# A 32-byte SBUF tensor is allocated ahead of the attention tensors instead of behind them, in a gated-attention and expert kernel

## The chip, the cores and the metric

The kernel runs as one program on one core of a Trainium2 chip. Its time is the device time of one execution in microseconds. Three executions took 1172.36, 1173.41 and 1173.3 us, median 1173.3 us.

## The reference: what is computed

`x` and `ctx_1024` are (8, 512, 512) float32: 8 batches of 512 rows, width 512. Two blocks follow each other, each added to its input.

```python
def xattn(char_emb, subword_emb, ...):            # char_emb = layernorm(x), subword_emb = ctx
    scores   = (char_emb Wq_c + bq_c)(subword_emb Wk_s + bk_s)^T / sqrt(512)
    char2sub = softmax(scores) (subword_emb Wv_s + bv_s)
    scores2  = (subword_emb Wq_s + bq_s)(char_emb Wk_c + bk_c)^T / sqrt(512)
    sub2char = softmax(scores2) (char_emb Wv_c + bv_c)
    gate = sigmoid([char2sub, sub2char] Wg^T + bg)
    return gate * char2sub + (1 - gate) * sub2char

def ffn(x, router_w, router_b, expert_w, expert_b):  # x = layernorm(x1), 4096 tokens, 8 experts
    probs = softmax(xt @ router_w + router_b)
    gate, idx = max(probs), argmax(probs)
    return gate * (xt @ expert_w[idx] + expert_b[idx])

x1  = x  + tanh(g_xattn) * xattn(layernorm(x), ctx, ...)
out = x1 + tanh(g_ffn)   * ffn(layernorm(x1), ...)
```

## The kernel before, in words

**Precision.** Every large product is made of three float32r matmuls, high times high, high times low and low times high (`PASSES`, L41, in `product`, L153 to L163). So each tensor that TensorE multiplies stands in SBUF as a pair of a high and a low part; ScalarE writes the high part out of PSUM, VectorE the low one.

**Stages.** First the query and key weights are multiplied with one another (`weights_part`), while the first rows of `x` are loaded into the tensor that the profile calls `pairs_as_f` (L689, L882). Four more weights follow, 128 rows at a time, through the two halves of `x1_tile` (L898 to L903). Then come 8 batches, the middle ones in a hardware loop; the order of each engine's work in a batch is written out by hand in `steps_of_a_batch` (L473 to L538). A batch has two directions of attention, each with four steps Q (queries), V (values), S (scores), PT (transposed probabilities) and U (the attended sum), then the gate product G, the mix M, and the router. Steps marked `prev` belong to the batch before, those marked `nxt` to the next one. Behind the last batch 39 tiles of 128 tokens go each through its own expert (`experts_part`): POOL gathers the rows of a tile from DRAM (L1617), SP loads the expert's bias, one row broadcast to 128 partitions (L1565), ScalarE normalises (L1655), TensorE transposes and multiplies (L1795, L160), VectorE adds (L1763, L1771), and POOL scatters the tile to the output (L1624).

**SBUF.** The program allocates SBUF tensors one behind the other in the order of the calls `sb(...)`, each rounded up to a multiple of 32 bytes per partition. Tensors opened on `top` keep their place to the end. The first group is the `arena` (nine slots for pairs of 512 by 512), constants, `in_tile` (three rows buffers of 2112 bytes), `junk`, `bn_x` and `mv_x` (L90 to L114). `attention_part` opens a second group behind them: `q_pair`, `c2s_pair`, `probs`, `x1_tile`, `diff`, `normed`, `normed_t`, then `row_next`, `bn_1`, `stats` and the small rest (L596 to L619). Two further names are other views of the same bytes: `pairs_as_f32` (L117) is opened and closed where `q_pair` and `c2s_pair` come to lie, and `experts_part` cuts its buffers out of these, of `probs`, of `in_tile` and of an arena slot (L1520 to L1531).

**The tensor of the change.** `row_next` has 8 float32 per partition. VectorE writes one element of it as the accumulated result of a dot product of a row with a vector, in steps XD (L1309 to L1311) and CD (L1316 to L1318), and copies all of it into `row_const` once in a batch (L1259). No other engine touches it.

**Who sets the order.** Semaphores alone: each step waits for counts that others raise. No scheduler or planner looks at the addresses.

Of the kernel before, what the change touches and what calls it, by code (L numbers as in the profile page):

```python
# [32 lines left out]
P = 128  # L33
B, L, H, E = 8, 512, 512, 8
C = H // P
T = L // P
# [37 lines left out]
def gated_attention_and_experts(nc, x, ctx_in, g_xattn, g_ffn, Wq_c, bq_c, Wk_s, bk_s, Wv_s, bv_s,  # L74
                                Wq_s, bq_s, Wk_c, bk_c, Wv_c, bv_c, Wg, bg, router_w, router_b,
                                expert_w, expert_b, out):
    x_rows = x.rearrange("b l h -> (b l) h")
    c_rows = ctx_in.rearrange("b l h -> (b l) h")
    out_rows = out.rearrange("b l h -> (b l) h")

    x1_dram = nc.dram_tensor("x1_rows", (N + 1, ROWX), F32, kind="Internal").ap()
    x1_early = nc.dram_tensor("x1_rows_early", (N - L, ROWX), F32, kind="Internal").ap()
    list_dram = nc.dram_tensor("token_lists", (SLOTS, LINE), I32, kind="Internal").ap()

    with ExitStack() as top:
        def sb(name, shape, dt=F32):
            return top.enter_context(nc.sbuf_tensor(name, shape, dt))


        k = Shared()  # L90
        with ExitStack() as scope:
            k.slot_as_f32 = [scope.enter_context(nc.sbuf_tensor(f"slot{i}_as_f32", [P, 2, C, H], F32)) for i in range(9)]
        k.arena = sb("arena", [P, 9, 2, C, H], F32R)
        k.ident = sb("ident", [P, P])
        k.ones_bf = sb("ones_bf", [P, P], BF16)
        k.before_bf = sb("before_bf", [P, P], BF16)
        k.u_row = sb("u_row", [P, 2, H])
        k.u_const = sb("u_const", [P, 2])
        k.c_col = sb("c_col", [P, 2, C])
        k.bv_col = sb("bv_col", [P, 2, C])  # L100
        k.bg_half = sb("bg_half", [P, C])
        k.tanh_g = sb("tanh_g", [P, 2])
        k.router_parts = sb("router_parts", [P, C, PARTS, E], BF16)
        k.router_b = sb("router_b", [P, E])
        k.rank_of_e = sb("rank_of_e", [P, E])
        k.list_start = sb("list_start", [P, E])
        k.list_end = sb("list_end", [P, E])
        k.tile_no = sb("tile_no", [P, TILES])
        k.minus_half = sb("minus_half", [P, 1])
        k.token_ids = sb("token_ids", [P, T + LINE - 1], I32)  # L110
        k.in_tile = sb("in_tile", [P, 3, ROWX])
        k.junk = sb("junk", [P, H], BF16)
        k.bn_x = sb("bn_x", [P, 6])
        k.mv_x = sb("mv_x", [P, 2, 3])  # L114


        with nc.sbuf_tensor("pairs_as_f32", [P, 2, 2 * C * L], F32) as pairs_as_f32:  # L117
            k.pairs_as_f32 = pairs_as_f32
        k.mm_bank, k.tr_bank, k.u_bank = (
            [top.enter_context(nc.psum_tensor(f"{name}{i}", [P, 512], F32)) for i in range(n)]  # L120
            for name, n in (("mm", 2), ("tr", 2), ("u", C)))
        weights = weights_part(nc, top, k, x1_dram, list_dram,
                               dict(Wq_c=Wq_c, bq_c=bq_c, Wk_s=Wk_s, bk_s=bk_s, bv_s=bv_s, Wq_s=Wq_s,
                                        bq_s=bq_s, Wk_c=Wk_c, bk_c=bk_c, bv_c=bv_c, bg=bg, g_xattn=g_xattn,
                                        g_ffn=g_ffn, router_w=router_w, router_b=router_b))
        with ExitStack() as scope:
            attention = attention_part(nc, scope, top, k, x_rows, c_rows, x1_dram, x1_early, list_dram, expert_w,
                                       (Wg[:, 0:H], Wv_s, Wv_c, Wg[:, H:2 * H]), weights)
        experts = experts_part(nc, top, k, x1_dram, x1_early, list_dram, out_rows, expert_b, attention)

        with nc.Block(no_gpsimd_drain=True) as block:
            @block.sync
            def _(sp):
                attention.sync(sp, weights.sync(sp), experts.sync(sp))

            @block.scalar
            def _(act):
                attention.scalar(act, weights.scalar(act), experts.scalar(act))

            @block.vector  # L140
            def _(dve):
                attention.vector(dve, weights.vector(dve), experts.vector(dve))

            @block.gpsimd
            def _(pool):
                attention.gpsimd(pool, weights.gpsimd(pool), experts.gpsimd(pool))

            @block.tensor
            def _(pe):
                attention.tensor(pe, weights.tensor(pe), experts.tensor(pe))  # L150
# [429 lines left out]
def attention_part(nc, scope, top, k, x_rows, c_rows, x1_dram, x1_early, list_dram, expert_w,  # L580
# [3 lines left out]
    bg_half, tanh_g, router_parts = k.bg_half, k.tanh_g, k.router_parts  # L584
    rank_of_e, list_end = k.rank_of_e, k.list_end
    minus_half, token_ids, in_tile = k.minus_half, k.token_ids, k.in_tile
    junk, bn_x, mv_x = k.junk, k.bn_x, k.mv_x

    def sb(name, shape, dt=F32):
        return scope.enter_context(nc.sbuf_tensor(name, shape, dt))  # L590
# [10 lines left out]
    diff = sb("diff", [P, H])  # L601
    normed = sb("normed", [P, H])
    normed_t = sb("normed_t", [P, 2, C, P], BF16)
    row_next = sb("row_next", [P, 2, T])
    bn_1 = sb("bn_1", [P, 6])
    stats_flat = sb("stats", [P, 4 * T + LINE - 4])
    stats = stats_flat[:, 0:4 * T].rearrange("p (t s) -> p t s", s=4)
# [1239 lines left out]
```

## Time and profile before

| | |
|---|---|
| median of 3 runs | 1173.3 us (1172.36 to 1173.41) |
| the profiled execution | 1172.36 us |
| its span, first to last instruction | 1170.6 us |
| outside the span | 1.76 us |
| TensorE busy | 1149.4 us, 98% of the span |
| VectorE, ScalarE, GpSimd busy | 712.3, 458.5, 212.8 us |
| granted TensorE clock, mean | 0.995 |

PE is TensorE's matmuls, PEld its weight loads, DVE VectorE, ACT ScalarE, POOL GpSimd, SP the engine that issues most DMAs. A name such as `x_tile` or `pairs_as_f` is the program's name with digits at the end of a part left out, so `x_tile` is `x1_tile`. A tensor that is seen through an alias is listed by the alias: the buffers of the expert stage appear as `pairs_as_f` (on the place of `q_pair` and `c2s_pair`) and as `slot_as_f` (on the arena). The share of DMA is the mean busy share of the core's 16 DMA engines.

### The profile page before, as it was taken

What the parts mean: (1) busy time and instruction counts of PE and PEld (TensorE: products, weight loads), DVE (VectorE), ACT (ScalarE), POOL (GpSimd) and SP (SyncE); (2) the same over time, 40 slices, a digit from 0 to 9 for tenths busy, and PEclk for the clock granted to TensorE, in tenths of its full rate; (3) what the DMA queues carried; (4) which work ended last, traced back from release to release, by engine and by line L of the source; (5) the groups of instructions that cost most, each with busy time, mean ns of one, the idle gap of its engine ahead of it and who ended that gap; (6) DMA issues with size and microseconds to landing.
All of it is one profiled execution on the core that took longest, in us unless ns stands there. A gap on an engine that the chain in (4) does not pass through costs nothing.

```text
span 1170.6 us, 18120 instructions
## 1 busy us (share of the span) xinstructions
PE 1149.4 (98%) x5937; PEld 944.7 (81%) x5937; DVE 712.3 (61%) x1497; ACT 458.5 (39%) x812; POOL 212.8 (18%) x339
## 2 busy tenths in 40 slices
PE   7999999999999999999999999999999999998998
PEld 6778888888888888888888888888888888877776
DVE  5765646565557545763566466646565658788565
ACT  5533423442344324432344244423442355544342
POOL 3300001010002100110011011201020101256664
PEclk8999999999999999999999999999999999999999
DMA  6042113010202020101101120102010312586683
GB/s 235 28 164 65 35 28 102 8 49 27 99 9 48 27 77 30 39 25 65 54 21 36 41 85 21 36 27 99 9 39 1 135 46 76 200 263 195 182 253 121
DMA packets 59445, 90.64 MB, mean 77 GB/s; under 512 B 20523, under 2 KB 21063, under 8 KB 59401
## 3 DMA queue, kind: packets, MB, share of 16 engines
q1 hardware_dynamic: 49232, 64.25, 18.0%
q0 software_dynamic: 7264, 19.20, 4.9%
q10 hardware_dynamic: 2904, 6.63, 1.5%
q8 instruction: 24, 0.39, 0.1%
q14 instruction: 21, 0.16, 0.0%
HBM read 62.77 MB, written 29.12 MB: 78 GB/s over the span
## 4 chain that ended last, share of the span: by engine, by line
PE 92%; issue 2%; DVE 2%; ACT 2%; another core or an unknown queue 1%; DMA 1%; POOL 1%; SPq 0%; POOLq 0%; DVEq 0%; ACTq 0%
PE mm L160 58%; PE u L1016 15%; PE tr L968 8%; PE u L160 7%; PE mm L1795 1%; PE tr L160 1%; PE tr L1070 1%; DVE arena L1238 1%; ACT pairs_as_f L1655 0%; DMA slot_as_f<-in_L_xattn_Wk_s 0%; ACT slot_as_f L281 0%; DMA x_tile<-in_L_xattn_Wv_s 0%; DVE arena L416 0%; POOL slot_as_f L346 0%
## 5 line engine op out<-in xcount | busy, mean ns | idle before, releaser
L160 PE MATMUL mm<-arena 128*128 128x512 f32 x1536 | 376.1, 396 | 1.9 <-DVE arena L1238 1.8
L160 PEld LDWEIGHTS mm<-arena 128*128 128x128 f32 x1536 | 284.3, 189 | 59.5 <-DVE arena L1238 2.2
L1016 PE MATMUL u<-arena 128*128 128x512 f32 x768 | 189.9, 398 | 0.0
L160 PE MATMUL mm<-arena,q_pair 128*128 128x512 f32 x768 | 183.8, 394 | 0.0
L160 PEld LDWEIGHTS mm<-arena,q_pair 128*128 128x128 f32 x768 | 141.7, 188 | 28.8
L1016 PEld LDWEIGHTS u<-arena 128*128 128x128 f32 x768 | 140.0, 188 | 27.5
L1238 DVE TENSOR_TENSOR arena<-tr,arena 128x512 fp32r<-128x512 f32 x144 | 96.3, 685 | 37.0 <-ACT arena L1131 16.9
L1238 DVE TENSOR_TENSOR arena<-mm,arena 128x512 fp32r<-128x512 f32 x64 | 44.2, 691 | 93.3 <-ACT arena L1122 89.2
L1118 ACT ACTIVATE q_pair<-mm,c_col 128x512 fp32r<-128x512 f32 x64 | 44.1, 689 | 125.9 <-PE mm L160 122.0
L1239 DVE SCALAR_TENSOR_TENSOR q_pair<-mm,c_col,q_pair 128x512 fp32r<-128x512 f32 x64 | 48.1, 751 | 72.9 <-ACT q_pair L1118 71.3
L1122 ACT ACTIVATE arena<-mm 128x512 fp32r<-128x512 f32 x64 | 38.3, 599 | 129.2 <-PE mm L160 129.2
L160 PE MATMUL mm<-c2s_pair,arena 128*128 128x512 f32 x360 | 87.2, 392 | 0.0
L160 PE MATMUL mm<-q_pair,arena 128*128 128x512 f32 x360 | 86.4, 389 | 0.0
L1127 ACT ACTIVATE probs<-mm,neg_top 128x512 f32<-128x512 f32 x64 | 44.2, 691 | 103.3 <-DVE neg_top L1265 95.0
L1422 POOL TENSOR_SCALAR mv_x<-mv_x 128x1 f32<-128x1 f32 x32 | 13.9, 435 | 381.7 <-DVE mv_x L1305 381.6
L160 PE MATMUL u<-arena,q_pair 128*128 x312 | 79.5, 405 | 1.9 <-DVE q_pair L1756 1.6
L160 PEld LDWEIGHTS mm<-q_pair,arena 128*128 128x128 f32 x360 | 67.6, 188 | 14.0
L160 PEld LDWEIGHTS mm<-c2s_pair,arena 128*128 128x128 f32 x360 | 67.1, 188 | 13.8
L1422 POOL TENSOR_SCALAR stats<-stats 128x1 f32<-128x1 f32 x32 | 7.9, 248 | 356.2 <-DVE stats L1337 356.0
L1284 DVE SCALAR_TENSOR_TENSOR probs<-probs,u 128x512 f32<-128x512 f32 x32 | 22.0, 687 | 79.7 <-ACT probs L1154 79.5
L160 PEld LDWEIGHTS u<-arena,q_pair 128*128 128x128 f32 x312 | 57.9, 192 | 13.9 <-issue 2.4
L1154 ACT ACTIVATE probs<-mm,bg_half 128x512 f32<-128x512 f32 x30 | 20.7, 690 | 123.6 <-PE mm L160 123.6
(213 smaller groups left out, 1558.6 us busy)
## 6 DMA issues: line engine op xcount, KB each, us to landing
in_tile<-in_ctx SPq DMA_DIRECT2D x31, 256.0 KB, 2.6
x_tile<-in_x SPq DMA_DIRECT2D x29, 256.0 KB, 2.6
x_rows<-x_tile SPq DMA_DIRECT2D x29, 256.0 KB
in_tile<-in_x SPq DMA_DIRECT2D x28, 256.0 KB, 2.7
x_rows_early<-x_tile SPq DMA_DIRECT2D x28, 256.0 KB, 2.3
probs<-in_L_ffn_expert_b SPq DMA_DIRECT2D x21, 256.0 KB
slot_as_f<-in_L_ffn_expert_w SPq DMA_DIRECT2D x4, 1024.0 KB, 5.2
slot_as_f<-in_L_ffn_expert_w ACTq DMA_DIRECT2D x3, 1024.0 KB, 8.9
```

Of the source, the lines that this page charges most:

```text
L160: last = pe.matmul(bank, lhsT(a, c), rhs(b, c), start=start and n == 0, stop=stop and n == C * len(PASSES) - 1)
L968: last = pe.transpose(bank[:, tile(n)], block_of(n), ident[:])
L1016: last = pe.matmul(u_bank[m][:], v_pair[:, i % 2, a, tile(m)], pt_pair[:, i % 2, p], start=i == 0 and n == 0, stop=i == T - 1 and n == 2)
L1070: last = pe.matmul(bank[:, 0:n * E], part_of_rows(i, part)[:, c], router_parts[:, c, 0:n].rearrange("p n e -> p (n e)"), start=c == 0 and ...
L1118: act.activation(q_pair[:, HI, i], bank[:], ACT.Identity, bias=c_col[:, d, i:i + 1]).then_inc(q_hi, 1)
L1122: act.activation(v_pair[:, i % 2, HI], bank[:], ACT.Copy).then_inc(v_hi, 1)
L1127: act.activation(probs[:, i], bank[:], ACT.Exp, bias=neg_top[:, d, i:i + 1], scale=SCALE, accum_out=p_sum[:, d, i:i + 1]).then_inc(exp_don ...
L1154: act.activation(probs[:, i], bank[:], ACT.Tanh, bias=bg_half[:, i:i + 1], scale=0.5).then_inc(tanh_done, 1)
L1238: return dve.tensor_tensor(to, bank, f32(hi), ALU.subtract)
L1239: return dve.scalar_tensor_tensor(to, bank, bias, f32(hi), ALU.add, ALU.subtract)
L1284: dve.scalar_tensor_tensor(mix, mix, 1.0, u_bank[i][:], ALU.subtract, ALU.mult).then_inc(nd_used, 1)
L1422: then(pool.tensor_scalar(rstd, var, EPS, None, ALU.add))
```

## The change

The call that allocates `row_next` moves from `attention_part`, where it stood behind `normed_t`, to the end of the first group, behind `mv_x`. `attention_part` takes it from there by its name.

```diff
@@ gated_attention_and_experts
         k.bn_x = sb("bn_x", [P, 6])
         k.mv_x = sb("mv_x", [P, 2, 3])
+        k.row_next = sb("row_next", [P, 2, T])
@@ attention_part
-    junk, bn_x, mv_x = k.junk, k.bn_x, k.mv_x
+    junk, bn_x, mv_x, row_next = k.junk, k.bn_x, k.mv_x, k.row_next
@@
     normed_t = sb("normed_t", [P, 2, C, P], BF16)
-    row_next = sb("row_next", [P, 2, T])
     bn_1 = sb("bn_1", [P, 6])
```

On every engine the same instructions stand in the same order as before, with the same shapes, waits and semaphores; only line numbers below L114 are one higher. What differs is the byte address, within each partition, of eight allocations (and of the alias `pairs_as_f32`):

| tensor | bytes | address before | address after | before, modulo 64 | after, modulo 64 |
|---|---|---|---|---|---|
| `q_pair`, `pairs_as_f32` | 16384, 32768 | 177280 | 177312 | 0 | 32 |
| `c2s_pair` | 16384 | 193664 | 193696 | 0 | 32 |
| `probs` | 8192 | 210048 | 210080 | 0 | 32 |
| `x1_tile` | 4096 | 218240 | 218272 | 0 | 32 |
| `diff` | 2048 | 222336 | 222368 | 0 | 32 |
| `normed` | 2048 | 224384 | 224416 | 0 | 32 |
| `normed_t` | 2048 | 226432 | 226464 | 0 | 32 |
| `row_next` | 32 | 228480 | 177280 | 0 | 0 |

All else stays: the arena at 16512, `in_tile` at 169856 (its three buffers begin at 0, 64 and 0 modulo 128), `bn_x` at 177216, `mv_x` at 177248, `bn_1` at 228512, and the small tensors behind it, among them `mx` at 228704 (32 modulo 64) and `neg_top` at 228736 (0 modulo 64). Before the change every one of the large tensors in the table begins at a multiple of 128 bytes, and so does each of the 2048-byte rows in them.

## Rows read from the trace of the kernel before

**Rows 1.** The page's head: span, and busy time of each engine.
```profile
span 1170.6 us, 18120 instructions
PE 1149.4 (98%) x5937; PEld 944.7 (81%) x5937; DVE 712.3 (61%) x1497; ACT 458.5 (39%) x812; POOL 212.8 (18%) x339
```
**Rows 2.** The chain that ended last, share of the span by engine.
```profile
PE 92%; issue 2%; DVE 2%; ACT 2%; another core or an unknown queue 1%; DMA 1%; POOL 1%; SPq 0%; POOLq 0%; DVEq 0%; ACTq 0%
```
**Rows 3.** Busy time by stretch; columns in the first row.
```profile
core 0: us, PE busy (x) PEld busy (x) DVE busy (x) ACT busy (x) POOL busy (x), PEclk, DMA share, GB/s
0.00:50.00 50.00, 42.19 (x195) 33.82 (x195) 32.66 (x59) 29.66 (x51) 19.96 (x42) 0.93 0.43 148
50.00:130.00 80.00, 78.64 (x394) 64.38 (x395) 50.69 (x112) 32.38 (x63) 1.66 (x4) 1.00 0.28 94
490.00:610.00 120.00, 120.00 (x631) 99.19 (x629) 69.65 (x151) 43.90 (x79) 12.81 (x28) 1.00 0.15 44
1000.00:1050.00 50.00, 48.87 (x253) 40.36 (x252) 40.57 (x66) 26.16 (x44) 18.80 (x22) 1.00 0.72 239
1050.00:1100.00 50.00, 44.09 (x252) 34.86 (x251) 35.77 (x83) 20.26 (x33) 32.23 (x32) 0.97 0.64 190
1100.00:1150.00 50.00, 49.30 (x245) 39.81 (x243) 32.68 (x47) 20.93 (x32) 31.88 (x31) 1.00 0.81 239
```
**Rows 4.** TensorE in order of time, gate and next Q: start, us, what.
```profile
288.57 2.88 PE L160 MATMUL mm<-c2s_pair,arena 128*128 128x512 f32 x12
291.29 2.88 PE L160 MATMUL mm<-q_pair,arena 128*128 128x512 f32 x12
294.01 8.33 PE L160 MATMUL mm<-arena 128*128 128x512 f32 x36
302.18 1.03 PE L968 MATMUL tr<-ident,probs 128*128 128x128 f32 x8
```
**Rows 5.** Matmul groups that read the shifted pairs: busy us, mean ns.
```profile
L160 PE MATMUL mm<-arena,q_pair 128*128 128x512 f32 x768 | 183.8, 394 | 0.0
L160 PE MATMUL mm<-c2s_pair,arena 128*128 128x512 f32 x360 | 87.2, 392 | 0.0
L160 PE MATMUL mm<-q_pair,arena 128*128 128x512 f32 x360 | 86.4, 389 | 0.0
```
**Rows 6.** Instructions on in_tile and pairs_as_f: ns min/median/max, first and last start.
```profile
L968 PEld LDWEIGHTS tr<-ident,in_tile x236: 137/139/143, 44.3 to 888.3; 128*128 128x128 f32 x118
L1655 ACT ACTIVATE pairs_as_f<-in_tile x21: 801/806/814, 1016.6 to 1158.2; 128x512 f32<-128x512 f32 x21
L1655 ACT ACTIVATE pairs_as_f<-pairs_as_f x18: 803/807/813, 1030.6 to 1148.6; 128x512 f32<-128x512 f32 x18
```
**Rows 7.** VectorE on small tensors, and what touches row_next.
```profile
L1263 DVE SCALAR_TENSOR_TENSOR mx<-mx,row_const 128x1 f32<-128x1 f32 x64 | 10.2, 159 | 2.2
L1265 DVE TENSOR_TENSOR neg_top<-row_const,mx 128x1 f32<-128x1 f32 x64 | 10.2, 160 | 2.2
L1309 DVE DVE_READ_ACCUMULATOR2_ANT row_next<- x32: 76/81/84, 44.2 to 891.0; 128x1 f32 x32
```
**Rows 8.** DMA issues: tiles, engine, count, KB each, us to landing.
```profile
in_tile<-in_ctx SPq DMA_DIRECT2D x31, 256.0 KB, 2.6
x_tile<-in_x SPq DMA_DIRECT2D x29, 256.0 KB, 2.6
probs<-in_L_ffn_expert_b SPq DMA_DIRECT2D x21, 256.0 KB
pairs_as_f<-in_L_ffn_expert_b SPq DMA_DIRECT2D x12, 256.0 KB
in_tile<-x_rows_early,u_row POOLq DMA_INDIRECT x11
pairs_as_f<-x_rows_early,u_row POOLq DMA_INDIRECT x9
```
**Rows 9.** Pieces of the chain in the expert stage.
```profile
1082.00 6.65 another core or an unknown queue
1096.80 3.46 another core or an unknown queue
```

## The prediction

> **What bounds the kernel now.** I read the page's head first, then the chain of waits, then the busy time by stretch, and last the single groups that touch what the change moves. The head says that TensorE is busy in 1149.4 us of a span of 1170.6 us [rows 1]. The chain agrees: 92% of it is TensorE [rows 2]. By stretch the reader is to see three regimes [rows 3]. From 0 to 50 us TensorE is busy for 42.19 us, from 50 to 130 us for 78.64 of 80 us. In the batches it has no gap at all (120.00 us of 120.00 between 490 and 610 us), with the DMA engines busy for only 0.15. From 1000 us the expert stage has few gaps but busy DMA engines: shares of 0.72, 0.64 and 0.81, and TensorE at 48.87, 44.09 and 49.30 of 50 us. So two things could move the end: a change in what a matmul costs, anywhere, or a change in what a transfer costs, in the expert stage. Everything else has cover.
>
> How matmuls follow one another is read from their starts, not from their durations, which overlap (the groups' means are 389 to 394 ns [rows 5]). Twelve matmuls with `c2s_pair` as moving operand start at 288.57, the next twelve, with `q_pair`, at 291.29, and the 36 that take both operands from the arena at 294.01 and end where the transposes start, at 302.18 [rows 4]. That is 2.72 us for 12, or 226.7 ns each, twice, and 8.17 us for 36, or 226.9 ns each. The pace is one and the same whatever tensor is streamed.
>
> **The change part by part.** No instruction is removed, added or reordered, and no wait changes. There are three things to price.
>
> (a) `row_next` itself moves. It is written by VectorE's accumulator reads (81 ns in the median of 32 [rows 7]) and copied once in a batch. These are writes of 4 bytes, and VectorE is busy for only 69.65 us of 120 in a batch's stretch [rows 3]. The nearest rows for the position of a small tensor are two operations on one element per partition: the one that writes `mx`, which begins at 32 modulo 64, takes 159 ns, the one that writes `neg_top`, at 0 modulo 64, takes 160 ns [rows 7]. The bound is 1 ns either way on 60 writes, 0.06 us, beside TensorE's work. I take 0. If the cover were gone it would still be 0.06 us.
>
> (b) The compute engines read and write `q_pair`, `c2s_pair`, `probs`, `x1_tile`, `diff`, `normed` and `normed_t` at 32 modulo 64 where it was 0. For VectorE and ScalarE I have rows at 0 and 64 modulo 128, since the three buffers of `in_tile` begin at both: ScalarE's normalisation out of it takes 801 to 814 ns over 21 cases, against 803 to 813 ns out of and into the aligned `pairs_as_f`, and TensorE's weight loads from it 137 to 143 ns over 236 [rows 6]. A residue by itself shows no effect there. No large tensor stands at 32 modulo 64 in this trace, so the price has to be bounded. The end above: if a row of 2048 bytes were fetched in pieces of 64 bytes, the shifted row would touch 33 of them where it touched 32, 1/32 more. For the 720 matmuls that stream `c2s_pair` or `q_pair` [rows 5] that is 720 x 226.7 / 32 = 5.1 us, all of it on the path, since TensorE has no gap there. The 768 that take `q_pair` as weights [rows 5] hide it: a weight load on `in_tile` is 139 ns [rows 6] beside a pace of 227 ns. The end below is a gain: in the gate product both operands begin at multiples of 128 now, so if that cost anything the shift would save it. But 226.7 and 226.9 ns are equal within 0.2 ns, with pairs of one kind or the other, and 0.2 x 720 = 0.14 us is what the rows let it be. Between +5.1 and -0.14 us I take 0, because every row that could show a dependence on the place shows none.
>
> (c) DMAs land in and leave shifted tensors. In the batches these are the residual loads and the stores of `x1_tile` at a DMA share of 0.15: loads into the aligned `x_tile` and into `in_tile`, with buffers at both residues, land in the same 2.6 us [rows 8]. They are issued several microseconds ahead and TensorE waits for none of them, so even a landing one half longer would cost nothing. At 50 to 130 us sixteen weight loads pass through `x1_tile`; the whole idle time of TensorE there is 1.36 us [rows 3]. In the expert stage a tile moves 264 KB of gathered rows, 256 KB of bias and 256 KB of output. Of the 39 biases 21 land in `probs` and 12 in `pairs_as_f` [rows 8], of the gathers those into `pairs_as_f` (9 from the early copy [rows 8] and 9 more), the output leaves the arena and does not move. So (33/39 x 256 + 18/39 x 264) / 776 = (217 + 122) / 776 = 0.44 of the bytes have a shifted end. The end below is 0. The end above, if a shifted packet took twice as long: the share of 0.81 becomes 0.81 x 1.44 = 1.17, and 50 us would need 58.3; 0.72 becomes at most 1.04, and 0.64 stays under 1 [rows 3]. That is +8.3 + 1.8, about +10 us at most. I take 0, as nothing shows such a price.
>
> By the Trainium skill, "DMA: Bandwidth & Descriptors", section on how a descriptor splits into AXI transactions, a source that does not begin at a multiple of 256 bytes is fetched from the boundary below it, in beats of 32 bytes. These rows begin 128 bytes past such a boundary before and 160 after, so by that rule a 2048-byte row read from SBUF costs 69 beats where it cost 68, 1.5% more, an estimate from the page. No row here shows a packet at the new residue, so the trace neither agrees nor disagrees. By the rule the sum would stay 0, but it speaks for a small price and against the doubling, and I lower the chance of the transfer case for it.
>
> **The sum.** Span 1170.6 + 0 + 0 + 0 = 1170.6 us, and 1.76 us around it make 1172.36, the profiled execution. The median of the runs is 0.94 us above that execution, so the forecast in the terms of the median is 1173.3 us.
>
> **The rivals.**
> *The transfers pay (slower).* Packets with a shifted end take much longer, and the expert stage, whose DMA engines are the busiest resource after TensorE, becomes bound by them. It decides from the point at which 0.81 x (1 + 0.44 a) = 1, a = 0.53: below a half more per packet the stretch of 1100 to 1150 us still fits. At a = 1 it costs +8.3 us there, 1181.6 us. For it: the share of 0.81, and two places where the chain hangs on something late at 1082 and 1096 us [rows 9]. Against it: in the rows at 0 and 64 modulo 128 there is no difference at all [rows 8].
> *The matmul stream pays (slower).* The 1/32 of (b), +5.1 us, 1178.4 us. For it: it would be on the path in full. Against it: it supposes pieces of 64 bytes, and TensorE's pace of 226.7 ns is the same in all streams [rows 4].
> *The late waits of the expert stage fall otherwise (faster).* Two pieces of the chain there, 6.65 and 3.46 us, are no engine's work [rows 9], and TensorE is idle for 5.9 us between 1050 and 1100 us [rows 3]. These come from how gathers, index loads and scatters meet in the queues. If the shift moves landings enough that the larger one doesn't occur, most of the 5.9 us comes back: say 4 us, 1169.3 us. Against it: with packet times unchanged there is nothing to move them, and the same lateness could as well grow.
> *The change does nothing of what it says.* It does move the addresses, but if addresses carry no price this is the forecast itself.
>
> **How the numbers follow.** I give the forecast 0.67: for it are all three prices of zero and an instruction stream that is the same. Transfers 0.10, the matmul stream 0.07, the faster expert stage 0.10, and 0.06 for a drift just past 0.2%, half to each side. A measurement of this kernel can tell about 0.2% (2.3 us) from no change. So faster 0.10 + 0.03 = 0.13, same 0.67, slower 0.10 + 0.07 + 0.03 = 0.20. The forecast's own range is 1171.5 to 1175 us. To hold 8 in 10 the range reaches to 1169.5, at the faster case, and to 1178.5, over the matmul case, and leaves out the doubled transfers.
>
> **What would show it.** In the profile after, the twelve-matmul groups of the gate should still start 2.72 us apart (a stream that pays shows 2.80), ScalarE's instruction of L1655, one line lower, should stay at 806 ns, loads into `x_tile` should land in 2.6 us, and the DMA share between 1100 and 1150 us should stay near 0.81. The forecast is wrong if TensorE's busy time changes by more than 2 us, if landings in shifted tensors lengthen while those in `in_tile` do not, or if the gaps of the expert stage change by more than 2.3 us.

## The result: slower by 0.8%, and the profile after

The changed kernel took 1184.59 us (median of 4 runs, 1183.26 to 1185.67) against 1173.36 us for the kernel before (4 runs, 1172.36 to 1174.52). The ratio is 1.0083 with a 95% interval of 1.0069 to 1.0096; it rests on all 21 executions of the changed kernel, whose median is 1182.87 us, so it is smaller than the quotient of the two medians just given (1.0096). The forecast was 1173.3 us, the range 1169.5 to 1178.5 us: the time lies outside. The profiled execution after took 1182.02 us, 9.66 us more than the one before (1172.36 us).

The page's head of the changed kernel, first the span, then busy time by engine, answers to [rows 1]:

```profile
span 1180.3 us, 18120 instructions
PE 1157.9 (98%) x5937; PEld 944.6 (80%) x5937; DVE 714.0 (60%) x1497; ACT 458.1 (39%) x812; POOL 209.5 (18%) x339
```

The instruction counts are the same. TensorE's busy time has grown by 8.5 us, the span by 9.7 us, and the other engines have stayed within 3.3 us. The granted clock is the same, 0.995 in the mean. By stretch, beside [rows 3] (columns: TensorE busy, weight loads, VectorE, ScalarE, GpSimd, clock, DMA share, GB/s):

```profile
490.00:610.00 120.00, 120.00 (x626) 98.32 (x625) 68.78 (x147) 43.47 (x79) 12.14 (x28) 1.00 0.13 42
1000.00:1050.00 50.00, 49.34 (x239) 40.40 (x238) 36.45 (x61) 24.20 (x41) 15.02 (x16) 1.00 0.61 194
1050.00:1100.00 50.00, 42.00 (x254) 33.03 (x254) 38.40 (x91) 21.66 (x35) 32.75 (x36) 0.97 0.67 212
1100.00:1150.00 50.00, 50.00 (x248) 40.90 (x247) 31.95 (x46) 19.52 (x30) 30.37 (x31) 1.00 0.79 236
```

TensorE had no gap in the batches before and has none now, at a granted clock of 1.00 both times, and yet 626 matmuls stand in 120 us where 631 stood. The stage of the experts comes about 9 us later than before, so its stretches don't hold quite the same work; none of them is bound by transfers. The DMA share from 1100 to 1150 us is 0.79, where it was 0.81, and TensorE has no gap there. Over the whole span TensorE's idle time is 22.4 us where it was 21.2 us (span less busy time). So most of the 9.7 us is matmuls of some kind that take longer. Which kind is read from the starts in order of time. This is the gate and what follows in the second batch, to be laid beside [rows 4] (start, us, what):

```profile
290.61 2.96 PE L161 MATMUL mm<-c2s_pair,arena 128*128 128x512 f32 x12
293.41 2.96 PE L161 MATMUL mm<-q_pair,arena 128*128 128x512 f32 x12
296.21 8.36 PE L161 MATMUL mm<-arena 128*128 128x512 f32 x36
304.41 1.03 PE L968 MATMUL tr<-ident,probs 128*128 128x128 f32 x8
308.83 11.44 PE L161 MATMUL mm<-arena,q_pair 128*128 128x512 f32 x48
```

Twelve matmuls that stream `c2s_pair` or `q_pair` against weights from the arena now start 2.80 us apart from the next twelve, 233.3 ns each, where it was 2.72 us and 226.7 ns. The 36 with both operands in the arena take 8.20 us from start to start, 8.17 before. The transposes of `probs`, which is also shifted, take 1.03 us for 8 as in [rows 4]. The 48 matmuls of the scores, with weights from `q_pair` and a stream from the arena, are slower too, 11.44 us. In the same view of the kernel before:

```profile
306.58 11.17 PE L160 MATMUL mm<-arena,q_pair 128*128 128x512 f32 x48
```

The pieces of the chain of waits (start, us) give the length of a batch, before and then after:

```profile
277.80 24.54 PE mm L160 x108
399.97 24.54 PE mm L160 x108
```
```profile
279.57 25.00 PE mm L161 x108
402.82 25.00 PE mm L161 x108
```

The 48 scores take 0.27 us more (11.44 against 11.17 us), 5.6 ns each. The same piece, 72 matmuls of the gate and the 36 behind them, comes back after 123.25 us where it came after 122.17 us: each batch is 1.08 us longer. Eight batches make 8.6 us.

**The sum of it.** The busy time of whole groups, beside [rows 5], gives what each kind costs over the run:

```profile
L161 PE MATMUL mm<-arena,q_pair 128*128 128x512 f32 x768 | 187.4, 399 | 0.0
L161 PE MATMUL mm<-c2s_pair,arena 128*128 128x512 f32 x360 | 89.3, 397 | 0.0
L161 PE MATMUL mm<-q_pair,arena 128*128 128x512 f32 x360 | 88.7, 395 | 0.0
```

The scores have grown from 183.8 to 187.4 us, by 3.6 us. That is less than 16 x 0.27 = 4.3 us, since only one direction's 48 run unbroken; the other direction's are cut up by transposes. The gate's two groups have grown by 2.1 and 2.3 us. To them belong 48 more gate matmuls of the last batch, which [rows 5] does not list, as they write to another PSUM bank. In the kernel before:

```profile
L160 PE MATMUL tr<-q_pair,arena 128*128 128x512 f32 x24 | 5.9, 395 | 0.0
L160 PE MATMUL tr<-c2s_pair,arena 128*128 128x512 f32 x24 | 5.6, 389 | 0.0
```

They now take 6.0 and 5.8 us. So the gate is 768 matmuls and costs 4.7 us more. The 468 matmuls of the expert stage with weights from the pairs have gone from 118.6 to 119.5 us, by 0.9 us. Together that is 9.2 us of the 9.7 us in the span; the batches' 8.6 us and the experts' 0.9 us make 9.5 us. Nothing else of size is needed. The rest stands where it stood: the weight loads of the scores and the gate take 188 ns before and after, ScalarE's instruction has a median of 808 ns (806 before), VectorE's reads of the accumulator one of 82 ns (81), and the loads into `in_tile` and `x1_tile` land in 2.6 us as before.

(In the changed kernel only lines 115 to 603 are one higher than before; from 604 on the numbers are the old ones. So ScalarE's instruction is still at L1655.)

### The profile page after: what moved, and what is told of

Same layout as the page of the kernel before. It is cut to its first block, busy times and chain, and to the rows that moved or that the text cites. A ratio compares the mean times of both kernels' runs of the same rounds, so it can differ in the third digit from the quotient of the medians.

```text
span 1180.3 us, 18120 instructions
## 1 busy us (share of the span) xinstructions
PE 1157.9 (98%) x5937; PEld 944.6 (80%) x5937; DVE 714.0 (60%) x1497; ACT 458.1 (39%) x812; POOL 209.5 (18%) x339
## 4 chain that ended last, share of the span: by engine, by line
PE 92%; DVE 3%; issue 2%; ACT 1%; DMA 1%; POOL 1%; SPq 0%; DVEq 0%; POOLq 0%; ACTq 0%
PE mm L161 58%; PE u L1016 15%; PE u L161 8%; PE tr L968 7%; PE mm L1795 1%; PE tr L161 1%; PE tr L1070 1%; DVE arena L1238 1%; DMA slot_as_f<-in_L_xattn_Wk_s 0%; DVE arena L417 0%; ACT slot_as_f L282 0%; DVE slot_as_f L1771 0%; DVE arena L401 0%; DMA x_tile<-in_L_xattn_Wv_s 0%; DVE slot_as_f L395 0%
## 5 line engine op out<-in xcount | busy, mean ns | idle before, releaser
L161 PE MATMUL mm<-arena,q_pair 128*128 128x512 f32 x768 | 187.4, 399 | 0.0
L1261 DVE TENSOR_REDUCE mx<-mm 128x1 f32<-128x512 f32 x64 | 44.3, 691 | 43.3 <-PE mm L161 40.0
```

The source lines that it names most:

```text
L161: last = pe.matmul(bank, lhsT(a, c), rhs(b, c), start=start and n == 0, stop=stop and n == C * len(PASSES) - 1)
L1261: then(dve.reduce_max(mx[:, d, i:i + 1], bank[:], axis=AX))
```

## The experiments

Two theories at the start. **A**: a row that does not begin at a multiple of 64 bytes costs TensorE time by itself, in the stream or as weights. **B**: only the distance between the place of the stream and that of the weights counts. The rival behind both was that transfers or other engines pay for the shifted tensors. "Distance" below is the address of the pairs less that of the arena, against the kernel before, where all rows of both begin at 128 modulo 256.

**all_32.** Everything is shifted by 32 bytes together (in the code cuts below, the removal of the old call is left out).

```diff
+        k.row_next = sb("row_next", [P, 2, T])
         with ExitStack() as scope:
             k.slot_as_f32 = ...
         k.arena = sb("arena", [P, 9, 2, C, H], F32R)
```

> row_next stands ahead of the arena, so the arena, in_tile and the pairs all begin at 32 modulo 64; the tensors of one matmul share their place again. Theory A (each 2048-byte or 512-byte row that begins off a multiple of 64 bytes costs 16 more cycles of TensorE's clock, whatever the other operand does): every one of the 4356 matmuls of 512 columns pays at least 6.7 ns, +29 us or more, 1202 us or above; Q steps slow from 2.72 us for 12 matmuls to 2.80 or more. Theory B (it is the difference in place between the operand that is streamed and the one that is loaded as weights that costs): no difference is left, 1173 us, 12 matmuls in 2.72 us everywhere.

Measured: 1173.09 us (10 runs), ratio 0.9986 (0.9975 to 0.9997) to 20 new runs of the kernel before (median 1174.74 us). The gate and the scores, in order of time:

```profile
287.93 2.88 PE L161 MATMUL mm<-c2s_pair,arena 128*128 128x512 f32 x12
290.65 2.88 PE L161 MATMUL mm<-q_pair,arena 128*128 128x512 f32 x12
305.95 11.17 PE L161 MATMUL mm<-arena,q_pair 128*128 128x512 f32 x48
```

2.72 us for twelve, though none of the tensors that TensorE multiplies here stands at a multiple of 64. Theory A is out, and it was A that the prediction's rival had priced. The move of `row_next` itself is out too, since it moves here as well.

**arena_32.** `row_next` ahead of the arena and `bn_1` behind `mv_x`: the arena at 32 modulo 64, the pairs back on a multiple of 64, 32 bytes between them.

> The arena and in_tile begin at 32 modulo 64, the pairs and everything behind them at 64 modulo 128. Theory A: Q, V and U pay with both operands, G as weights and S as the stream, again +27 us or more, about 1200 us; of the single-operand cases S should show 2.80 us for 12 (the streamed operand pays) and G about 2.78 (the weights pay). Theory B: only S, G and the expert products pay, as in the changed kernel, so 1183 to 1185 us, with Q, V and U at 2.72 us for 12.

Measured: 1182.42 us (4 runs), ratio 1.0061 (1.0044 to 1.0078). The same view:

```profile
289.57 2.96 PE L162 MATMUL mm<-c2s_pair,arena 128*128 128x512 f32 x12
292.37 2.96 PE L162 MATMUL mm<-q_pair,arena 128*128 128x512 f32 x12
295.17 8.36 PE L162 MATMUL mm<-arena 128*128 128x512 f32 x36
307.79 11.44 PE L162 MATMUL mm<-arena,q_pair 128*128 128x512 f32 x48
```

The same 2.80 us and 11.44 us as in the changed kernel, while Q and V, both of whose operands are now shifted, pay nothing. B holds, A would have asked for 1200 us.

**rest_32.** The pairs stay, the rest is shifted.

```diff
     c2s_pair = sb("c2s_pair", [P, 2, C, L], F32R)
+    row_next = sb("row_next", [P, 2, T])
     probs = sb("probs", [P, T, L])
```

> row_next stands between c2s_pair and probs: the pairs stay at multiples of 128, and only probs, x1_tile, diff, normed and normed_t are shifted by 32 bytes. Both theories on TensorE's operands say 1173 us, within 0.2%. The rival, that transfers into and out of shifted tiles or the other engines pay, says that a good part of the 10 us is here: 1178 us or more.

Measured: 1174.08 us (10 runs), ratio 0.9991 (0.9979 to 1.0002). The shift of `probs`, `x1_tile`, `diff`, `normed` and `normed_t`, with every transfer into and out of them, costs nothing that can be measured. The transfers into the two pairs are not in this run; they are in all_32, which is no slower either.

**pairs_64.** The changed kernel with `bn_1` behind `row_next`: distance 64.

> As the changed kernel, with 32 more bytes ahead of q_pair, so that q_pair, c2s_pair, probs, x1_tile, diff and normed are shifted by 64 bytes against the kernel before. If the unit is 64 bytes (both theories in their first form): 1173 us and 2.72 us for 12 matmuls of the gate. If the unit is 128 bytes or the shift itself costs: 1183 to 1185 us.

Measured: 1179.91 us (5 runs, 1178.0 to 1182.14), ratio 1.0041 (1.0024 to 1.0057), between the two answers that were expected.

```profile
291.08 2.91 PE L162 MATMUL mm<-c2s_pair,arena 128*128 128x512 f32 x12
293.82 2.91 PE L162 MATMUL mm<-q_pair,arena 128*128 128x512 f32 x12
309.20 11.45 PE L162 MATMUL mm<-arena,q_pair 128*128 128x512 f32 x48
```

Here the two kinds part: the gate's groups are 2.74 us apart, near the old 2.72, and the scores take 11.45 us, as in the changed kernel. So the unit is not 64 bytes. In the gate the stream lies above the weights, in the scores below them, so the sign of the distance may be what parts them. That is not isolated: the two steps also read in a different order, and at 32 bytes both signs cost nearly the same.

**pairs_16, pairs_96, pairs_128, pairs_256.** In the first the two pairs are slices of one allocation, 16 bytes in; in the others two, three and seven more small tensors (`bn_1`, `row_const`, `mx`, ...) are allocated behind `row_next`. Of the edit for 16 bytes the cut shows the main part; `pairs_as_f32` moves with it, and two small tensors are joined.

```diff
-    q_pair = sb("q_pair", [P, 2, C, L], F32R)
-    c2s_pair = sb("c2s_pair", [P, 2, C, L], F32R)
+    both = sb("both_pairs", [P, 4 * C * L + 8], F32R)
+    q_pair, c2s_pair = (both[:, 4 + n * 2 * C * L:4 + (n + 1) * 2 * C * L].rearrange(...) for n in range(2))
```

> q_pair and c2s_pair are slices of one allocation, 16 bytes past a multiple of 128; probs and what follows is at 32 modulo 64, which cost nothing where it was tried alone. The difference in place between the arena and the pairs is 16 bytes. If only the difference modulo 64 or 128 counts and each difference but zero costs about the same: 1183 us, 12 matmuls of the gate in 2.80 us. If the cost grows with the difference and 32 is its height: between 1176 and 1181 us. If differences below 32 bytes are free: 1174 us and 2.72 us.

> row_next, bn_1 and row_const stand ahead of q_pair: pairs and what follows is 96 bytes on. Difference to the arena 96 bytes, that is 32 modulo 64 and -32 modulo 128. If the unit is 64 bytes: as the changed kernel, 1183 us and 2.80 us for 12 matmuls of the gate. If differences count modulo 128 with their sign, the cost can be another: between 1174 and 1190 us.

> row_next, bn_1, row_const and mx stand ahead of q_pair: pairs and what follows is 128 bytes on. If the cost repeats every 128 bytes: 1174 us and 2.72 us for 12, as before. If it follows the difference over a longer stretch: another time, 1177 us or more, and a pace in the gate or the scores other than 226.7 ns.

> Eight small tensors stand ahead of q_pair: pairs and what follows is 256 bytes on. If the cost repeats every 128 or 256 bytes: 1174 us and 2.72 us for 12. If the shift of 128 bytes costs and this one doesn't, the period is 256; if both cost, it is longer. No theory says that this one is cheap and the one of 128 bytes is dear unless the period is 256.

TensorE in order of time at distances 16, 96, 128 and 256, a piece of the gate and then the score step:

```profile
284.83 9.66 PE L160 MATMUL mm<-both_pairs,arena 128*128 128x512 f32 x41
294.33 8.35 PE L160 MATMUL mm<-arena 128*128 128x512 f32 x36
...
306.92 11.13 PE L160 MATMUL mm<-arena,both_pairs 128*128 128x512 f32 x48
```
```profile
292.48 2.96 PE L163 MATMUL mm<-c2s_pair,arena 128*128 128x512 f32 x12
295.28 2.96 PE L163 MATMUL mm<-q_pair,arena 128*128 128x512 f32 x12
310.69 11.49 PE L163 MATMUL mm<-arena,q_pair 128*128 128x512 f32 x48
```
```profile
290.55 2.95 PE L164 MATMUL mm<-c2s_pair,arena 128*128 128x512 f32 x12
293.34 2.94 PE L164 MATMUL mm<-q_pair,arena 128*128 128x512 f32 x12
308.74 11.40 PE L164 MATMUL mm<-arena,q_pair 128*128 128x512 f32 x48
```
```profile
289.48 2.88 PE L168 MATMUL mm<-c2s_pair,arena 128*128 128x512 f32 x12
292.20 2.88 PE L168 MATMUL mm<-q_pair,arena 128*128 128x512 f32 x12
307.49 11.17 PE L168 MATMUL mm<-arena,q_pair 128*128 128x512 f32 x48
```

All distances in one table. The gate column is the step from the start of one group of 12 to that of the next (at 16 the groups have one name, and it is 12/41 of the 9.50 us from 284.83 to 294.33 us), the scores column is the duration of 48.

| distance, bytes | kernel | median, us | ratio (95%) | gate, 12 | scores, 48 |
|---|---|---|---|---|---|
| 0 | before | 1173.36 | 1 | 2.72 us | 11.17 us |
| 0 | all_32 | 1173.09 | 0.9986 (0.9975 to 0.9997) | 2.72 | 11.17 |
| 16 | pairs_16 | 1179.93 | 1.0048 (1.0031 to 1.0064) | 2.78 | 11.13 |
| 32 | changed | 1184.59 | 1.0083 (1.0069 to 1.0096) | 2.80 | 11.44 |
| 32 | arena_32 | 1182.42 | 1.0061 (1.0044 to 1.0078) | 2.80 | 11.44 |
| 64 | pairs_64 | 1179.91 | 1.0041 (1.0024 to 1.0057) | 2.74 | 11.45 |
| 96 | pairs_96 | 1183.87 | 1.0076 (1.0053 to 1.0098) | 2.80 | 11.49 |
| 128 | pairs_128 | 1181.38 | 1.0057 (1.0037 to 1.0076) | 2.79 | 11.40 |
| 256 | pairs_256 | 1174.7 | 1.0005 (0.9992 to 1.0017) | 2.72 | 11.17 |

Each ratio is to the kernel before as it ran beside that run (medians 1174.74 us for all_32, arena_32 and pairs_64, 1174.43 us for the other four of this series). The intervals of the runs at 32, 96 and 128 bytes overlap; the times alone don't rank them.

A distance of 256 bytes is as good as none, one of 128 is not: the cost repeats after 256 bytes and not after 128. pairs_256 also contains the whole change under study, with `row_next` ahead of `q_pair`, and has nothing of its cost. That all distances repeat so is not shown; 256 is the one point tried.

At 16 the time lies in the range that was expected if the cost grows with the distance, but the two kinds part: the gate pays 5 ns a matmul, the unbroken 48 scores nothing. The scores of the other direction do pay, though. First the kernel before, then pairs_16:

```profile
237.54 5.74 PE L160 MATMUL mm<-arena,q_pair 128*128 128x512 f32 x24
```
```profile
237.36 5.85 PE L160 MATMUL mm<-arena,both_pairs 128*128 128x512 f32 x24
```

In the changed kernel this group takes 5.84 us. So at 16 bytes the same distance with the same sign costs as much as 32 bytes in one group and nothing in another, and something besides the distance decides there.

**alternate and alternate_0.** Which weights must agree with a stream: those of its own matmul, or those of the next, which are loaded while it streams? 144 extra matmuls stand behind the last tile.

```diff
+            elif kind == "END":
+                pe.wait_ge(e_out, TILES)
+                # W, S: weights and stream from the arena; w, s: from q_pair
+                blocks = ([(W, S)] * 24, [(W, s)] * 24, [(w, S)] * 24, [(w, s)] * 24, [(W, s), (w, S)] * 24)
+                for block in blocks:
+                    for n, (lhsT, rhs) in enumerate(block):
+                        pe.matmul(y_bank[0][:], lhsT(n), rhs(n), start=n == 0, stop=n == len(block) - 1)
```

> The changed kernel, with 144 further matmuls of 512 columns behind the last tile, whose results nobody reads: 24 with weights and stream from the arena, 24 with arena weights and a stream from q_pair, 24 the other way round, 24 with both from q_pair, and 48 that alternate between (arena weights, q_pair stream) and (q_pair weights, arena stream). The second and third groups should start about 233 ns apart, the first and the fourth 227. Theory C (the loss comes from a matmul's stream read beside the load of the NEXT matmul's weights): in the alternating 48 each stream meets weights from its own tensor, so they start 227 ns apart. Theory D (it is a matmul's own weights and own stream whose places must agree): all 48 have them apart, so 233 ns.

> The same 144 matmuls behind the kernel before, where arena and pairs share their place modulo 256: every group starts 227 ns apart by both theories. If the alternating group is slower here, alternation has a cost of its own.

On the changed kernel's addresses (one run, 1213.03 us):

```profile
1183.02 5.77 PE L1828 MATMUL u<-q_pair,arena 128*128 128x512 f32 x24
1188.62 5.75 PE L1828 MATMUL u<-arena,q_pair 128*128 128x512 f32 x24
1194.21 5.63 PE L1828 MATMUL u<-q_pair 128*128 128x512 f32 x24
1199.68 0.39 PE L1828 MATMUL u<-q_pair,arena 128*128 128x512 f32 x1
...
1202.24 0.39 PE L1828 MATMUL u<-arena,q_pair 128*128 128x512 f32 x1
...
1204.54 0.39 PE L1828 MATMUL u<-arena,q_pair 128*128 128x512 f32 x1
```

On those of the kernel before (one run, 1204.55 us):

```profile
1175.11 5.60 PE L1828 MATMUL u<-q_pair,arena 128*128 128x512 f32 x24
1180.55 5.60 PE L1828 MATMUL u<-arena,q_pair 128*128 128x512 f32 x24
1185.99 5.60 PE L1828 MATMUL u<-q_pair 128*128 128x512 f32 x24
1191.43 0.39 PE L1828 MATMUL u<-q_pair,arena 128*128 128x512 f32 x1
...
1202.08 0.39 PE L1828 MATMUL u<-arena,q_pair 128*128 128x512 f32 x1
```

With equal places each of the three groups of 24 shown takes 5.44 us from start to start, 226.7 ns each, and the alternating 48 keep that pace (47 steps from 1191.43 to 1202.08 us), so alternation has no cost of its own. The first 24, all from the arena, follow a wait and are not compared. With 32 bytes between the tensors the mixed 24 take 5.60 and 5.59 us, 233 ns each, but 5.47 us where both operands are from `q_pair`. So the effect stands alone, with the other compute engines done and no batch around it, and 32 bytes cost the same in both directions.

The alternating 48 start, after the first few, 230 ns apart (ten steps from 1202.24 to 1204.54 us), midway: neither C's 227 nor D's 233. The same trace also holds the weight loads (PEld), named by the operands of the matmul that they are for:

```profile
1202.01 0.39 PE L1828 MATMUL u<-q_pair,arena 128*128 128x512 f32 x1
1202.01 0.19 PEld L1828 LDWEIGHTS u<-arena,q_pair 128*128 128x128 f32 x1
```

While a stream from `q_pair` runs, the weights of the next matmul are loaded, also from `q_pair`, and the record of that load ends before the next stream starts at 1202.24 us. This is the overlap that C supposes, and still 3.3 ns of the loss remain. So neither theory holds in its simple form, and which meeting of reads costs the time stays open.

## Why the prediction was wrong

**What bounds the kernel** was right: TensorE without a gap in the batches, and a price on a matmul goes straight into the time.

**Step (a)**, `row_next` itself at 0, was right: all_32 and pairs_256 move it and are no slower.

**Step (b) failed.** It took 0 for the compute engines, between +5.1 and -0.14 us, "because every row that could show a dependence on the place shows none". Those rows could not show it. The streams compared in [rows 4], from the arena and from the pairs, all ran against weights whose rows begin at the same place modulo 256, so that they were the same case three times. What would have had to be varied is the place of one operand against that of the other, and no large matmul of the trace did that. The step went wrong in its ceiling as well. It priced the stream alone, 5.1 us for 720 matmuls (with the 48 of the last batch it would have been 5.4 us), and the gate did cost 4.7 us, by the very sign the prediction had named (2.80 us for twelve). But it let the 768 matmuls with weights from `q_pair` go free, as hidden behind the stream: they cost 3.6 us, and the 468 of the expert stage, which it didn't price, another 0.9 us. The 139 ns it set beside 227 were those of a transpose's load; the loads of these matmuls take 188 ns. Either way the length of a weight load, which the change left alone, says nothing about what the place of the weights does to the stream.

By the Trainium skill, "SBUF — State Buffer", section "Who interferes with whom", TensorE reads the stream and the weights through two independent ports and never waits on anyone. The measurement decides otherwise: the pace of a matmul depends on where its two operands lie against each other, 226.7 ns at a distance of 0 and 256 bytes, 233.3 ns at 32. The rival of step (b), fetches in pieces of 64 bytes, gave nearly the right price of the gate for a wrong reason: all_32 has every row off a multiple of 64 and pays nothing.

**Step (c)** was right with 0, and the transfer rival, at 0.10, was wrong though its 1181.6 us was the nearest to the time: rest_32 is at 0.9991, the loads into `in_tile` and `x1_tile` land in 2.6 us as before, and the DMA share did not rise where it was highest (0.79 after 0.81 between 1100 and 1150 us). A number near the result is no evidence for its mechanism.

**The faster rival** did not occur: TensorE's gap between 1050 and 1100 us grew from 5.9 to 8.0 us, while the stretches before and behind it lost 0.5 and 0.7 us of theirs. Since the stage also comes later, these are not the same tiles.

**The chances.** 0.20 for slower rested on the fact that no instruction changes. An identical instruction stream fixes what is done, not how fast; with TensorE at 98% and some 4400 matmuls of 512 columns, 1 ns on each is 4.4 us, nearly twice what the measurement can tell, and the chance had to be set by that.

## What to carry to other kernels

Where TensorE is the bound, it is worth placing the tensors that meet in one matmul so that their rows begin at the same place modulo 256 bytes; a 32-byte tensor allocated ahead of one of them and not of the other cost 3% of each such matmul here. Small tensors then belong behind the large ones, or are padded to 256 bytes in sum. These runs show it for float32r matmuls of 128 by 512 columns back to back; other types and shapes are not measured. When a change alters addresses only, compare pairs of operands by their distance, not each tensor by its own alignment.

## What the runs showed of the hardware that was not expected

The pace of float32r matmuls of 128 by 512 columns, at the full granted clock, depends on the distance between the stream's row and the weights' row: 226.7 ns at a distance of 0 or 256 bytes, 233.3 ns with the stream 32 bytes above the weights, 228 to 229 ns at 64, 232 to 233 ns at 128. The step from 226.7 to 233.3 ns is 6.6 ns, 16 cycles at 2.4 GHz (worked out). At 32 bytes the sign hardly counts (5.60 and 5.59 us for 24). At 64 bytes the gate pays 2 ns and the scores as much as at 32, and at 16 bytes some groups pay and others don't, so the distance alone does not give the pace there. The weight loads of the scores and the gate last 187 to 189 ns at every distance that was tried, so the loss doesn't show in them. Eight transposes of 128 columns out of the shifted `probs` take 1.03 us, as before. Why the distance matters inside the memory was not measured.
